# Picked rows in place of all four experts' rows in the third layer's projection of an eight-stage GNN/MoE kernel, with the record moves dealt out anew

## The reference

```python
x = x + L0_gnn(layernorm(x)); x = x + L0_ffn(layernorm(x))
x = x + L1_gnn(layernorm(x)); x = x + L1_ffn(layernorm(x))
x = x + L2_gnn(layernorm(x)); x = x + L2_ffn(layernorm(x))
x = x + L3_gnn(layernorm(x)); x = x + L3_ffn(layernorm(x))
```

```python
scores = _layernorm(agg, ln_gamma, ln_beta).reshape(M, HEADS, NUM_EXPERTS).mean(1)
topk_s, topk_i = jax.lax.top_k(scores, TOP_K)
w = jax.nn.softmax(topk_s, axis=-1)
for ei in range(NUM_EXPERTS):
    g = jnp.where(topk_i == ei, w, 0.0).sum(-1)
    hh = jax.nn.gelu(x @ W1[ei] + b1[ei], approximate=False)
    out = out + g[..., None] * (hh @ W2[ei] + b2[ei])
```

## Time and profile before

| | us |
|---|---|
| median of three runs | 8807.85 |
| the profiled execution, its own time | 8805.21 |
| its span | 8803.1 |
| `m0_proj` (first record move to the next phase's first DMA) | 2258.1 to 2505.6 |
| `m0_ffn` | 2505.6 to 2999.2 |
| `l1_proj` | 2999.2 to 3148.9 |
| `gat_proj` | 4238.2 to 4351.6 |
| `gat_scores` | 5901.3 to 5926.3 |
| `l2_proj` | 5934.4 to 6192.7 |
| TensorE, VectorE, POOL busy | 5993.1, 5511.9, 5197.2 |
| mean granted TensorE clock | 0.83 of full |

### The profile page before, as it was taken

The page is one execution under the profiler, slowest core; times in us unless marked ns, Lnnn a source line. Parts: engine busy times, 40 slices in busy tenths (PEclk is TensorE's granted clock), DMA queues, the critical chain, the costliest instruction groups (busy, mean ns, idle before and its releaser), DMA issues. The chain is left out here.

```text
span 8803.1 us, 115446 instructions
## 1 busy us (share of the span) xinstructions
PE 5993.1 (68%) x29150; PEld 4494.9 (51%) x29150; DVE 5511.9 (63%) x14431; ACT 3064.8 (35%) x8921; POOL 5197.2 (59%) x5085
## 2 busy tenths in 40 slices
PE   0266787775259766656598999974477775574499
PEld 0133555553248534444477777763355553453487
DVE  8787888887656566665544434346577777435444
ACT  0111888886422210000233333321244444313322
POOL 0274666665567667777577777742677771433422
PEclk9687999998579987777699989877689886786699
DMA  9412655665147533333111111116433344463364
GB/s 303 152 52 80 172 172 170 175 174 150 37 152 213 163 99 101 101 102 102 35 28 30 26 29 31 26 27 200 115 103 104 104 102 116 155 214 91 115 199 163
DMA packets 655611, 1031.12 MB, mean 117 GB/s; under 512 B 134978, under 2 KB 462066, under 8 KB 654780
## 3 DMA queue, kind: packets, MB, share of 16 engines
q0 software_dynamic: 238656, 527.35, 22.3%
q1 hardware_dynamic: 390636, 444.00, 16.0%
q10 hardware_dynamic: 25744, 53.10, 2.0%
HBM read 806.11 MB, written 225.75 MB: 117 GB/s over the span
## 5 line engine op out<-in xcount | busy, mean ns | idle before, releaser
L4092 POOL DMA_INDIRECT gat_edges_rows<-gat_table,gat_room x1080 | 1171.4, 1085 | 366.4 <-issue 327.9
L2570 POOL DMA_INDIRECT l_edges_ring<-pairs,first_room x832 | 841.8, 1012 | 525.6 <-issue 243.1
L2132 POOL DMA_INDIRECT l_sum_rows<-l_feats,back_room x832 | 826.7, 994 | 279.8 <-issue 241.9
L2152 PE MATMUL l_sum_o<-l_sum_rows,l_sum_s 128*128 128x256 f32 x1664 | 616.2, 532 | 442.3 <-DVE l_sum_s L2163 206.2
L2621 ACT ACTIVATE l_edges_ring<-l_edges_ring,l_edges_weight 128x64 f32<-128x64 f32 x3328 | 816.5, 336 | 0.0
L2152 PEld LDWEIGHTS l_sum_o<-l_sum_rows,l_sum_s 128*128 128x128 f32 x1664 | 416.3, 264 | 635.8 <-DVE l_sum_s L2163 306.6
L2693 PE MATMUL l_edges_o<-l_edges_ring,l_edges_sf 128*128 128x260 f32 x1664 | 534.5, 427 | 148.8 <-DVE l_acc L2826 140.9
L3723 ACT ACTIVATE m_ffn_ht<-m_ffn_hp,m_ffn_b1t 128x256 f32<-128x256 f32 x592 | 280.7, 475 | 868.4 <-PE m_ffn_hp L3691 868.1
L2174 DVE TENSOR_TENSOR l_acc<-l_acc,l_sum_o 128x256 f32 x832 | 350.0, 421 | 346.6 <-PE l_sum_o L2152 256.6
L3701 PE MATMUL m_ffn_yp<-m_ffn_w2b,m_ffn_ht 128*128 128x256 f32 x2368 | 546.6, 384 | 29.2 <-ACT m_ffn_ht L3723 28.5
L3691 PE MATMUL m_ffn_hp<-m_ffn_xt,m_ffn_w1b 128*128 128x256 f32 x2368 | 548.7, 385 | 5.8 <-DVE m_ffn_xt L3738 3.0
(11 more groups left out here) (868 smaller groups left out, 14612.4 us busy)
## 6 DMA issues: line engine op xcount, KB each, us to landing
sorted_rows<-count_main_zero ACTq DMA_DIRECT2D x1, 51858.0 KB, 237.8
l_proj_taken<-m_by_node SPq DMA_DIRECT2D x56, 768.0 KB, 7.4
m_ffn_xs<-sorted_rows SPq DMA_DIRECT2D x144, 258.0 KB, 3.5
m_ffn_w1b<-in_L_ffn_w SPq DMA_DIRECT2D x32, 1024.0 KB, 6.2
m_ffn_w2b<-in_L_ffn_w SPq DMA_DIRECT2D x32, 1024.0 KB, 5.1
m_ffn_w1b<-in_L_ffn_W SPq DMA_DIRECT2D x56, 512.0 KB, 4.5
m_ffn_w2b<-in_L_ffn_W SPq DMA_DIRECT2D x56, 512.0 KB
m_by_node<-gat_edges_ys SPq DMA_DIRECT2D x96, 256.0 KB
```

Of the source, the lines that this page charges most:

```text
L2132: pool.indirect_dma_start(rows[:, slot, j, :], None, table, bass.IndirectOffsetOnAxis(ap=L.src[:, t:t + 1], axis=0)).then_inc(got[slot], 16)
L2152: pe.matmul(o[:, j, 0:D], s4[:, q % S4, j, :], rows[:, slot, j, :], start=True, stop=True).then_inc(out_done, 1)
L2570: pool.indirect_dma_start(rows(q, 0, 2 * D)[:, j, :], None, table, bass.IndirectOffsetOnAxis(ap=L.src[:, t:t + 1], axis=0)).then_inc(got[q ...
L4092: pool.indirect_dma_start(rows[:, slot, j, :], None, table, bass.IndirectOffsetOnAxis(ap=L.src[:, q * B + j:q * B + j + 1], axis=0)).then_ ...
```

## The change

`l2_proj` gets another front, `PickFront`. `gat_scores` now also writes, for each node and each of its two choices, the row number expert*T*P + node as int32 into the unused half of the weight table, and writes the two softmax weights directly. POOL gathers the two rows of each node by indirect DMA, 14 for a chunk, 98 in all, into one of three buffers, with a wait from chunk 3 on that chunk c-3 has been added. VectorE adds two rows a tile in place of four. SP loads nothing for the front. `measured` falls from 4 to 2, so `late` from 12 to 10. In this phase POOL carries 4 quads: chunks 0 and 1 are gathered, the records' fetch is waited for, and then chunk c is followed by the quads (c-2)*4//5 up to (c-1)*4//5, one each after chunks 3, 4, 5 and 6.

```diff
-MOVES = (3, 6, 58, 8, 5, 16, 54, 22, 14, 10)
+MOVES = (3, 6, 58, 8, 5, 2, 62, 27, 21, 4)
...
+class PickFront(Front):
+    measured = 2
...
+    def room(self, ph):
+        self.rows = ph.sb("picked", [P, 3, 2, CH, D])
+        self.got = [ph.gathered_sem(k) for k in range(3)]
...
+    def gather(self, pool, c, bound):
+        if c >= 3:
+            pool.wait_ge(self.second_added, (c - 2) * CH)
+        pool.sem_inc(self.taken, 1)
+        for j in range(CH):
+            for k in range(2):
+                pool.indirect_dma_start(self.rows[:, c % 3, k, j, :], None, self.by_node,
+                                        bass.IndirectOffsetOnAxis(ap=self.row[:, c * CH + j, k:k + 1], axis=0)
+                                        ).then_inc(self.got[c % 3], 16)
...
+    def work(self, dve):
+        def first(t, par):
+            c = t // CH
+            if t % CH == 0:
+                dve.wait_ge(self.got[c % 3], 32 * CH * (c // 3 + 1))
+            self.add(dve, t, 0).then_inc(self.first_added, 1)
+        def second(t, par):
+            dve.wait_ge(self.first_added, t + 1)
+            self.add(dve, t, 1).then_inc(self.second_added, 1)
+        return [(0, first), (1, second)]
...
+            elif carrier and front:
+                @block.gpsimd
+                def _(pool):
+                    front.gather(pool, 0, None)
+                    front.gather(pool, 1, None)
+                    carrier.start(pool)
+                    for c in range(2, T // CH):
+                        front.gather(pool, c, None)
+                        carrier.move(pool, (c - 2) * carrier.quads // (T // CH - 2), (c - 1) * carrier.quads // (T // CH - 2))
...
 in gat_scores:
+                o.then(dve.tensor_scalar(node[:], core.row[:, 0:T], float(P), core.part[:], ALU.mult, ALU.add))
...
-                    o.then(dve.tensor_tensor(chosen[:, k], names, per_node(first[:]), ALU.is_equal))
+                    o.then(dve.tensor_scalar(first[:], first[:], float(H - 1), None, ALU.min))
+                    o.mark(dve.scalar_tensor_tensor(out=row[:, :, k], in0=first[:], scalar=float(T * P), in1=node[:],
+                                                    op0=ALU.mult, op1=ALU.add))
                     if k == 0:
-                        o.then(dve.tensor_scalar(apart[:], chosen[:, k], -1.0, 1.0, ALU.mult, ALU.add))
+                        o.then(dve.tensor_tensor(apart[:], names, per_node(first[:]), ALU.not_equal))
                         o.then(dve.tensor_tensor(left[:], left[:], apart[:], ALU.mult))
-                        o.then(dve.scalar_tensor_tensor(out=left[:], in0=chosen[:, k], scalar=-FAR, in1=left[:],
-                                                        op0=ALU.mult, op1=ALU.add))
+                        o.then(dve.tensor_scalar(apart[:], apart[:], FAR, -FAR, ALU.mult, ALU.add))
+                        o.then(dve.tensor_tensor(left[:], left[:], apart[:], ALU.add))
...
-                o.then(dve.reciprocal(share[:, 0], first[:]))
-                o.then(dve.tensor_tensor(share[:, 1], diff[:], share[:, 0], ALU.mult))
-                o.mark(dve.tensor_tensor(left[:], chosen[:, 0], per_node(share[:, 0]), ALU.mult))
-                o.then(dve.tensor_tensor(apart[:], chosen[:, 1], per_node(share[:, 1]), ALU.mult))
-                dve.tensor_tensor(weight[:], left[:], apart[:], ALU.add)
+                o.then(dve.reciprocal(weight[:, :, 0], first[:]))
+                o.mark(dve.tensor_tensor(weight[:, :, 1], diff[:], weight[:, :, 0], ALU.mult))
```

More of the change, by code:

```diff
@@ new lines, in add @@
+    def add(self, dve, t, k):
+        c, j, n = t // CH, t % CH, LAST if t == T - 1 else P
+        x = self.core.x[0:n, t, :]
+        return dve.scalar_tensor_tensor(out=x, in0=self.rows[0:n, c % 3, k, j, :], scalar=self.weight[0:n, t, k:k + 1],
+                                        in1=x, op0=ALU.mult, op1=ALU.add)
+    def work(self, dve):
+        def first(t, par):
[7 more added lines that the diff above has]
+        return [(0, first), (1, second)]
@@ L4434, in _, with gat_scores @@
                 act.activation(flat(ex[:]), flat(ex[:]), ACT.Exp).then_inc(done, 1)
-def gat_scores(nc, core, acc, scores, w, weight):
+def gat_scores(nc, core, acc, scores, w, weight, row):
     H, C = 4, 4
@@ L4454, in gat_scores @@
         best = ph.sb("best", [P, 2, T])
-        share = ph.sb("share", [P, 2, T])
-        chosen = ph.sb("chosen", [P, 2, T, H])
+        node = ph.sb("node", [P, T])
         diff = ph.sb("diff", [P, T])
```

40 lines of the change are left out of this document (8 added, 32 removed).

## The result

| | before | after |
|---|---|---|
| median of the runs | 8805.86 us (8800.45 to 8810.25) | 8750.01 us (8732.84 to 8761.94) |
| span of the profiled execution | 8803.1 us | 8730.7 us |
| mean granted clock of TensorE | 0.830 | 0.838 |

The ratio is 0.9937, with a 95% interval of 0.9926 to 0.9948. The kernel became faster by 56 us in the medians; 8746 was forecast, in a range of 8716 to 8776. The time came from where the forecast had it, but not in its sizes. A phase's length here runs from the first DMA that SP issues in it to the first of the next phase; m0_ffn and gat_edges are taken from a DMA 2.4 and 0.4 us behind their first, in every kernel alike, and l2_proj is taken with the small turn of its weights ahead of it.

The account below looks back on a forecast made before the run. No one engine bounds the kernel, since every phase ends in a barrier; in l2_proj VectorE waits for stores behind SP's loads. Terms -57 -19 +5 +5 +4 = -62 take 8805.2 to 8743, plus 2.6 for the median: 8746 us, range 8716 to 8776.

Parts of the forecast that it names:

- The store wait: l2_proj: VectorE waits 13.39 us for stores queued behind 3.5 MB of SP's loads; all such waits 65.6 us, going with the loads.
- l2_proj, -57: l2_proj: 110 POOL issues at 1.32 us bound the phase; last copy at 6128 in place of 6185.3, 57 us gained.
- The forecast's own better end: l2_proj: at 1.25 us an issue POOL is no longer alone as the bound, and the gain is about 64 us.
- Rival (d): l2_proj: store wait stays, as gathers share the DMA engines with the stores; gain some 10 us, kernel 8793; chance 0.04.
- Rival (a): POOL's queue in l2_proj: gathers at 1.84 us or more lose its whole gain; at 1.97 the kernel takes 8817; chance 0.04.
- m0_proj, -19: m0_proj: 40 moves fewer save POOL 50 us, but it then waits for z's chain at 25.4 us a chunk; 19 gained.
- Rival (c): m0_proj: POOL held the chain all along, so its saving comes out nearly whole; -89 in all, kernel 8719; chance 0.09.
- m0_ffn, +5: m0_ffn: 36 us of added moves fit 34 us of POOL's idle time; last run's extra quad costs 5, between 0 and 16.
- l1_proj, +5: l1_proj: 20 more moves at 1.29 us end at 3148.7, with 6 more 3154.7 for 3149.6; 5 us lost, 0 to 8.
- gat_proj, +4: gat_proj: 28 more moves at 1.28 us end at 4350.6, with 6 more 4356.6 for 4352.4; 4 us lost, 0 to 8.
- the 6 us from there to the next phase: l1_proj and gat_proj: from the last move's end to the next phase 6 us, taken from 7.5 us behind m0_ffn's last store.
- the backlog rival: Backlog in m0_ffn, full costs in three phases: +16 +8 +8, 12 in m0_proj, 50 in l2_proj; -30, 8778; chance 0.13.

Follow-up runs that it names:

- e5: Kernel before, with the loads of chunks 2 to 6 in l2_proj issued by ScalarE and not by SP; 8782.56 us, ratio 0.9968.
- e4: Kernel before with all its loads in l2_proj, but VectorE adds only experts 0 and 1, two adds a tile; 8762.93 us, ratio 0.9943.
- e6: Changed kernel with another deal: quads m0_proj 10 (8 before the first scatter), m0_ffn 60, l1_proj 25, gat_proj 19, l2_proj 2; 8725.78 us, ratio 0.9908.
- e7: Changed kernel with e6's deal, but 61 quads in m0_ffn and one in l2_proj, after its last gather; 8725.01 us, ratio 0.9903.
- e8: Changed kernel with e6's deal, but m0_ffn 57 quads and m0_proj 13, one in each of rounds 2 to 6; 8715.13 us, ratio 0.9897.
- e11: e8 with m0_ffn's quads rounded up, so that the double quad stands in the first run and not the last; 8710.47 us, ratio 0.9887.
- e10: Changed kernel with m0_ffn's 62 quads rounded up, so the first run carries a double quad and the last a single; 8744.24 us, ratio 0.9927.

## Why the prediction was right, and where its terms were off

**The forecast held** (8746 against 8750.0 and, a second time, 8750.2), and in the main by its own mechanism. Much of the closeness is luck. The five touched phases gave 49 us in both profiled executions, where 62 was the sum: three phases cost 21 us more than their terms, two gained 9 more. The medians differ by 56, and what the other 7 are isn't known beyond the interval of the ratio (46 to 65 us). The range isn't made as the text says: its ends take -32 for m0_proj and +7 and +20 for the three phases, which aren't the bounds stated for them. With those (-50 and 0, +32) it would have been 8694 to 8784, and the result lies in both.

**The store wait.** That VectorE waits for stores and not for the loaded rows was read rightly, and so was that the wait goes with the loads. That the stores "queue behind them" was not shown: in e5 stores land as late with the loads in another queue (7.2 us against 6.6). Half of the wait was SP issuing the loads, half the landing beside them. And the adds were as much a part of the period as the wait (e4). The forecast needed only that all of it go.

**l2_proj, -57, measured -62.7.** Relative to the phase's start, the last copy came 5.2 us earlier than the sum had it. By its steps: the first gather starts 0.7 us behind SP's first DMA and not 0.3, 110 issues took 142.2 us and not 145.2 (1.29 for 1.32), from there to VectorE's next add it is 2.9 and not 1.4, and from that add to the last copy 42.7 and not 47. The last is mostly a miscount: `late` falls by 2, and 19 copies stand behind that add in the trace, where the sum took 20 steps. The forecast's own better end, 64 at 1.25 us with POOL no longer alone as the bound, is what e6 and e7 show: at the changed kernel's 12 moves POOL is the bound only just. Rival (d), the store wait that stays, falls: no wait before a copy is over 2.7 us.

**Rival (a)** had its place right and its price absent: 0.984 us beside adds of 0.472. The 3100 ns that the Trainium skill, "SBUF — State Buffer", on the trap in which DVE blocks DMA, gives beside a VectorE `tensor_copy` show in no gather here: the longest of the 98 takes 1.42 us. But the page speaks of VectorE operations in a 2-port mode, a float32 copy from SBUF to SBUF for one. Here VectorE ran adds of two SBUF operands and copies out of PSUM, and whether any of them is of that kind no run shows; the runs show only that no wait of that size stood in this phase.

**m0_proj, -19, measured -22.** The chain's pace was 25.2 us a chunk and not 25.4, and its last z came 6.9 us earlier in the phase, not 2.9 (98 transposes from 2253.5 to 2415.8, against the earlier trace rows). What stood behind it was priced well. Rival (c), a chain held by POOL so that its saving comes out nearly whole, falls: POOL waits in every chunk, the chain gained 4 us beyond the forecast's 3, and 11 quads more than the changed kernel's 2 fit in for nothing (e8).

**m0_ffn, +5, measured +16: the step that failed.** The text set 34 us of slack against 36 us of added moves, called it "just that", and charged the last run's extra quad only. The runs show four parts, in the sum up to the last store, which came 13.7 us later in the phase:

- 28 moves more, 36 us, as priced. The last run's quad among them did cost 5 (e11 against e8: 5.1).
- POOL's 360 instructions of the phase each took a little longer (moves 0.993 for 0.981 us, stores 1.050 for 1.032), together 5 us. This was put at nothing.
- Of the 34 us of slack 28 were used. The other 6 lie almost all before the first double run, the tenth, where there was no backlog that could have used them.
- The first store came 0.8 us later.

Beyond the last store the phase closes 2.5 us later, 10.0 for 7.5. Without the last run's quad and this some 9 us are backlog that was never worked off, and VectorE waits for it (99.7 us in e10; with 57 quads that wait is gone). The upper bound given, 16, is what came.

**l1_proj, +5, measured +11; gat_proj, +4, measured +8.** The last moves end where the text had them to within 0.2 us: 149.5 us into l1_proj both times, and 4351.6 where 4350.6 and a start 1.2 us later make 4351.8. What failed is the 6 us from there to the next phase: it takes 11.5 and 9.3. The row it was taken from was the 7.5 us behind `m0_ffn`'s last stores, shortened because the rows moved are small; the runs show it longer behind an unbroken run of moves. In l1_proj a part of the 11 may be the short execution of the kernel before (see the result). The Trainium skill, "Perfetto Trace Analysis", on the DMA instruction of SWDGE, says that the end shown for one is when its descriptors are written and not when the data has landed. The end that the trace shows for a last move thus isn't the end of its work; how the 11.5 us divide between landing, the waits for it and the phase's clearing was not measured.

The chances: 8778 (the backlog rival, -30) was wrong in l2_proj and m0_proj and near in the other three, where it had +16, +8 and +8 and +16, +11 and +8 came.

## What to carry to other kernels

A store that is late has two times to look at: when it was issued, and how long it took to land. The first shows what its issuing engine was busy with before it, the second what the DMA engines carried beside it, and another queue mends the first alone. Add up what lies in a ring one behind the other, since what is taken from each part of it adds up. Before work is moved onto an engine "with slack", find where in time the slack lies, and which instruction is last before the phase's end: of an idle time of 34 us in sum 28 could be used, and one quad in the last run cost its full 5. When a deal of work is changed together with the code that needs it, run the two apart; here the deal alone lost 13 us, and a better one won some 40 more.

## What the runs showed of the hardware

- Behind back-to-back moves of POOL the next phase began 11.5 us (l1_proj) and 9.3 us (gat_proj) after the last one's shown end, the same in all four kernels with these counts. Behind m0_ffn's last two stores it was 7.5 with 54 quads (six kernels), 8.5 and 8.8 with 57, 9.8 and 9.3 with 60 and 61, and 10.0 with 62. Why it grows isn't shown: the pauses before the last stores are the same with 54 quads and in e11 with 57.
- Issuing eight loads of 3.5 MB in all holds the issuing engine: the first five take 0.4 to 0.7 us each, later ones up to 2.15 us on SP (kernel before, the loads from 5984.54) and 3.46 on ScalarE (e5, from 6023.68). ScalarE can't compute meanwhile, for 9.4 us there. The last chunk's loads hold SP for 13.2 us (from 6094.28).
- A store of 128 KB that runs beside loads of 3.5 MB landed 6.6 us after its issue with both in SP's queue and 7.2 us with the loads in ScalarE's, against 2.6 us with no loads under way (e5). All the same VectorE's longest wait before a copy out of PSUM was 1.8 us in e5 and 20.8 in the kernel before: there SP issued no store for 7.0 us a chunk, and for 13.2 in the chunk of the 20.8.
- gat_edges with the two small phases behind it took between 1563.8 and 1578.3 us in the profiled executions, though no edit touches gat_edges; the granted clock in it was 0.91 in the shortest and 0.88 in the longest. That is as much as many an effect that one would want to see.
